# Output projection of a fused cross-attention and FFN kernel by seven block products per head pair, with its sums placed among the softmax steps

## What is computed

```python
x = x + xattn(layernorm(x), ctx, Wq, Wk, Wv, Wo)      # Wo: (16*128, 512)
#   scores = q k^T / sqrt(128); attn = softmax(scores); out = (attn v) @ Wo
x = x + ffn(layernorm(x), w_gate, w_up, w_down)       # silu(gate) * up, then down
```

## Time and profile before

| | us |
|---|---|
| median of 3 runs (lowest to highest) | 2036.09 (2035.24 to 2036.58) |
| the profiled execution: time / span in the profile | 2035.61 / 2034.0 |
| PE busy | 2016.0 (99%) |
| DVE / ACT / POOL busy | 1528.0 (75%) / 1001.8 (49%) / 739.9 (36%) |
| DMA, mean | 95 GB/s |

### The profile page before, as it was taken

How to read it: one execution, slowest core, us unless ns; L and a number is a source line. 1 busy time by engine, 2 the same in 40 slices (tenths; PEclk the granted TensorE clock), 3 DMA queues, 4 the chain that set the end, 5 groups by cost and what they waited for, 6 DMA issues and landing times.

```text
span 2034.0 us, 44904 instructions
## 1 busy us (share of the span) xinstructions
PE 2016.0 (99%) x15422; PEld 1508.8 (74%) x15422; DVE 1528.0 (75%) x3341; ACT 1001.8 (49%) x2679; POOL 739.9 (36%) x877
## 2 busy tenths in 40 slices
PE   8999999999999999999999999999999999999999
PEld 6888878788888887878888888888888885444444
DVE  6767777777777777777777777776656557899886
ACT  8955554554555545545554555545555443333332
POOL 5413333332333233333333333322111104878776
PEclk9999999999999999999999999999999999999999
DMA  8834344444444444444444354534233354555555
GB/s 253 219 63 92 83 97 87 84 92 91 88 89 91 92 91 86 87 89 91 87 81 102 73 105 77 104 71 94 53 84 58 68 133 98 91 87 94 93 91 99
DMA packets 456111, 193.74 MB, mean 95 GB/s; under 512 B 419456, under 2 KB 432256, under 8 KB 455904
## 3 DMA queue, kind: packets, MB, share of 16 engines
q1 hardware_dynamic: 433984, 140.31, 36.3%
q0 software_dynamic: 15584, 44.45, 8.8%
q10 hardware_dynamic: 6336, 6.29, 1.0%
HBM read 61.21 MB, written 27.26 MB: 43 GB/s over the span
## 4 chain that ended last, share of the span: by engine, by line
PE 93%; DVE 2%; DMA 2%; ACT 1%; issue 1%; POOL 0%; DVEq 0%; ACTq 0%; SPq 0%; POOLq 0%
PE b_qk L1085 33%; PE b_v L1085 17%; PE b_c L1085 10%; PE b_s L1085 9%; PE b_o L1140 8%; PE b_w L1140 8%; PE b_o L1211 3%; PE b_w L1211 2%; PE b_pt L1085 2%; PE b_x L1085 2%; DMA probT<-psplit 1%; ACT psplit L663 0%; DVE nmax L917 0%; ACT prob L653 0%; DVE kvT L755 0%
## 5 line engine op out<-in xcount | busy, mean ns | idle before, releaser
L1085 PE MATMUL b_qk<-kvT,attn_weights 128*128 128x256 f16 x3072 | 377.2, 273 | 3.7 <-DVE qk L755 2.9
L1085 PE MATMUL b_v<-attn_weights,kvT 128*128 128x256 f16 x3072 | 377.2, 273 | 0.0
L1085 PE MATMUL b_qk<-xT,attn_weights 128*128 128x256 f16 x3072 | 377.2, 273 | 0.0
L653 ACT ACTIVATE prob<-b_s,nmax 128x256 f32<-128x256 f32 x514 | 239.3, 470 | 278.2 <-DVE nmax L917 276.3
L1085 PEld LDWEIGHTS b_qk<-kvT,attn_weights 128*128 128x128 f16 x3072 | 300.2, 98 | 92.9 <-issue 5.1
L944 DVE SCALAR_TENSOR_TENSOR psplit<-prob,rrec,psplit 128x256 f16<-128x256 f32 x514 | 306.0, 636 | 79.6 <-ACT psplit L663 79.6
L755 DVE SCALAR_TENSOR_TENSOR qk<-b_qk,qk 128x512 f16<-128x512 f32 x256 | 176.7, 690 | 246.0 <-ACT qk L609 236.0
L609 ACT ACTIVATE qk<-b_qk 128x512 f16<-128x512 f32 x256 | 152.6, 596 | 423.4 <-PE b_qk L1085 423.0
L1085 PEld LDWEIGHTS b_qk<-xT,attn_weights 128*128 128x128 f16 x3072 | 300.6, 98 | 34.8
L1085 PEld LDWEIGHTS b_v<-attn_weights,kvT 128*128 128x128 f16 x3072 | 300.6, 98 | 34.8
L663 ACT ACTIVATE psplit<-prob,rrec 128x256 f16<-128x256 f32 x514 | 233.3, 501 | 69.2 <-DVE rrec L937 69.2
(11 more groups left out here) (131 smaller groups left out, 2685.8 us busy)
## 6 DMA issues: line engine op xcount, KB each, us to landing
ffn_w<-wffn SPq DMA_DIRECT2D x48, 256.0 KB, 2.8
acc<-xtok POOLq DMA_DIRECT2D x16, 512.0 KB, 4.7
out<-acc POOLq DMA_DIRECT2D x16, 512.0 KB, 3.3
xrow<-xtok POOLq DMA_DIRECT2D x31, 256.0 KB, 3.1
kvrow<-kvt POOLq DMA_DIRECT2D x61, 128.0 KB, 2.4
out<-attn_weights POOLq DMA_DIRECT2D x28, 256.0 KB, 5.4
stage<-wattn SPq DMA_DIRECT2D x12, 512.0 KB, 4.4
ffn_scratch<-ffn_t SPq DMA_DIRECT2D x48, 128.0 KB, 2.4
```

Source lines behind the costliest of these rows:

```text
L653: last = eng.activation(half(prob, q, 256), half(bS, q, 256), ACT.Exp, bias=nmax[:, q:q + 1], scale=1.0, accum_out=rsum[:, q:q + 1])
L1085: last = eng.matmul(out, l, r, start=(a == 0), stop=(a == len(pairs) - 1))
```

## The change

Pairs u = 0 to 15 (batches 0 and 1) are projected as before. From u = 16 (`FAST = 2`) a pair's product, (256 tokens x 256) times (256 x 512), is taken as a 2x2 block product and made from seven block products, each 128x128 times 128x256, instead of eight, from sums and differences of blocks (`TERMS`, m1 to m7). The parts:

- **PE**: `project_fast`: m1, m3, m4, m2 in even steps (12 matmuls of 256 columns into `b_pt` and `b_x`), m5, m7, m6 in odd steps (9, into `b_o` and `b_w`). A pair is projected one step later than before. The first pair of a batch from batch 3 waits by product for the sums of the previous batch (`m_step`, `READ`).
- **Left operand**: ACT leaves the context in fp32 (`evict_rows`), POOL forms five sums of blocks per pair (`left_sums`), ACT their hi (`left_hi`, 896 columns), DVE their lo (`left_lo`, 896 columns). Context lo per head goes away.
- **Right operand**: once, in quads 4 to 7: each of eight weight blocks is loaded, summed (POOL), split (ACT, DVE: `out_lo`) and stored in DRAM as 128x3584 fp16. Two blocks stay in SBUF after that, six per batch are loaded again (`load_slot`, 128x2048 and 128x1536), behind softmax transposes on SP's queue.
- **Sums into the rows**: 12 additions of 256 columns per batch (`add_products`) in place of two of 512, in groups of four behind the row maximum of heads 1, 2 and 3 of q = 1. For the last batch one addition per v = 0..11 of the FFN stage.
- **Moved**: FFN weight rounding runs in quads 8 to 55 (was 4 to 51); in q = 1 `ffn_magic` stands in head 3 (was 2); `x1_stats` stands in q = 2, head 1 (was q = 1, heads 2 and 3); `tile_rstd`, `store_x1`, `x_rescale` later in POOL's order. In the FFN stage two bank pairs serve until u = 27 (was 3), three after; ten downs stand at the end (was eight). SP's loops are written out.

```diff
+THIRD = 28
-GU_BUF = [u % 2 if u < 4 else (u - 2) % 3 for u in range(2 * PAIRS)]
+GU_BUF = [u % 2 if u < THIRD else (u - THIRD + 2) % 3 for u in range(2 * PAIRS)]
-NO_DOWN = (0, 1, 2, 3, 36, 40, 44, 48)
+NO_DOWN = (0, 1, 2, 3, 44, 47, 50, 53, 56, 59)
+TERMS = (("m1", "a0+b1", 3), ("m3", "a0", 2), ("m4", "b1", 1), ("m2", "a1+b1", 0)), \
+    (("m5", "a0+b0", 4), ("m7", "b0-b1", 6), ("m6", "a0-a1", 5))
+READ = {"m1": 4, "m3": 4, "m4": 8, "m2": 8, "m5": 11, "m7": 11, "m6": 12}
...
@@ gpsimd
+            def left_sums(n, k):
+                wait_apart(eng, "c_hi", 4 * n + k + 1)
...
+                eng.tensor_tensor(blocks[:, 4:6, :], blocks[:, 1:9:7, :], blocks[:, 0:4:2, :], ALU.add)
+                eng.tensor_tensor(blocks[:, 6:8, :], blocks[:, 0:2, :], blocks[:, 2:9:6, :], ALU.subtract)
+                eng.tensor_tensor(blocks[:, 3, :], blocks[:, 1, :], blocks[:, 2, :], ALU.add)
...
@@ scalar
+            def left_hi(n, k):
+                u = 2 * n + k // 2 - 2 - FAST_PAIR
+                eng.wait_ge(sm["s_sum"], 3 * (u + 1))
...
+                eng.activation(left_part(k // 2, 0).rearrange("p (n f) -> p n f", f=P), blocks[:, 1:8, :], ACT.Copy,
+                               scale=1.0).then_inc(sm["s_hi"], 1)
@@ vector
+            def left_lo(n, k):
+                eng.wait_ge(sm["s_hi"], 2 * n + k // 2 - 1 - FAST_PAIR)
+                eng.tensor_tensor(left_part(k // 2, 1).rearrange("p (n f) -> p n f", f=P), blocks[:, 1:8, :],
+                                  left_part(k // 2, 0).rearrange("p (n f) -> p n f", f=P), ALU.subtract
+                                  ).then_inc(sm["s_lo"], 1)
...
+            def add_products(b, group):
...
+                if group == 1:
+                    add_product(b, "m4", 1, 0, 0, 1)
+                    add_product(b, "m4", 1, 1, 0, None)
+                    add_product(b, "m2", -1, 1, 1, 4)
+                    add_product(b, "m2", 1, 1, 0, 6)
...
             def quad(...):
...
-                    if front or k < 3:
+                    sums = q == 1 and (not isinstance(s, int) or s > FAST)
+                    if sums and k > 0:
+                        add_products(s - 1, k - 1)
+                    if q == 2 and k == 1 and (not isinstance(s, int) or s > 0):
+                        for j in range(2):
+                            x1_stats(s - 1, j)
+                        x1_aggr(s - 1)
+                    if (front or k < 3) and not fast(n, k, 3):
...
-                    if ffn and k == 2:
+                    if ffn and k == 2 + sums:
                         ffn_magic(w)
...
@@ tensor
+            def project_fast(u, part):
...
+                for name, rows, block_ in TERMS[part]:
+                    at = LEFT[rows] * P
+                    if first_ and batch > FAST:
+                        eng.wait_ge(sm["m_step"], 12 * (batch - 1 - FAST) + READ[name])
+                    for z, (a, b) in enumerate(PARTS):
+                        last = eng.matmul(product_at[name], left_part(u % 2, a)[:, at:at + P], slot_w(slot, block_, b), ...)
@@ sync
+                    if QPB <= n < 2 * QPB and k % 2:
+                        j = 2 * (n - QPB) + k // 2
+                        store_out(j)
+                        if j < 7:
+                            load_out(j + 1)
+                    fill(i)
```

More of the change, by code:

```diff
@@ L366, in load_x_tile @@
                                         ).then_inc(sm[f"xqT_loaded{at}"], 16)
-            for n in range(NQ - 4, NQ - 1):
-                ffn_quad(n, store=False, load=False)
-            for k in range(QUAD):
-                transpose_p(4 * (NQ - 1) + k, k % 2)
-                if k < 2:
-                    load_x_tile(k, k)
+            begin = {0: 2 * 1 + 6, 4: 2 * 3 + 6, 1: 2 * 5 + 6, 2: 2 * 6 + 6}
+            fills = {}
+            for p_, step in begin.items():
+                for part in range(2):
+                    fills.setdefault(FAST_HEAD - 16 + step + part, []).append((FAST_PAIR + p_, part, FAST_HEAD - 20 + step))
@@ new lines, in _, with fill @@
+            order = [u for u in range(FAST_PAIR, B * H // 2) if u % 8 in RING]
+            for at, u in enumerate(order[2:]):
+                for part in range(2):
+                    old = order[at]
+                    fills.setdefault(2 * old + 6 + part, []).append((u, part, 2 * old + 1 + part))
+            def fill(i):
+                for u, part, done in fills.get(i, ()):
+                    eng.wait_ge(sm["o_done"], done)
+                    load_slot(u, part)
+            for n in range(NQ):
+                for k in range(QUAD):
+                    i = 4 * n + k
+                    w = n - FFN_FROM
+                    transpose_p(i, k % 2)
+                    if n % 2 and k == 1 and n < NQ - 4:
+                        transpose_x(n // 2)
+                    if n < QPB:
+                        for g in (EARLY + PIECES * n + 2 * k, EARLY + PIECES * n + 2 * k + 1):
+                            if PIECES <= g < QPB * PIECES - SLOTS:
+                                reload(g)
+                    if i == 4 * QPB - 1:
+                        load_out(0)
+                    if QPB <= n < 2 * QPB and k % 2:
[4 more added lines that the diff above has]
+                    fill(i)
+                    if i == 4 * FFN_FROM - 1:
+                        load_ffn(0)
+                    if FFN_FROM <= n < FFN_TO - 1 and k == 1:
+                        eng.wait_ge(sm["ffn_y"], w + 1)
+                        load_ffn(w + 1)
+                    if FFN_FROM < n <= FFN_TO and k == 2:
+                        transpose_ffn(w - 1)
+                    if FFN_FROM < n <= FFN_TO and k == 3:
+                        store_ffn(w - 1)
+                    if n == NQ - 1 and k < 2:
+                        load_x_tile(k, k)
@@ L374, in _ @@
             transpose_p(4 * NQ, 0)
+            fill(4 * NQ)
+            fill(4 * NQ + 1)
             def transpose_inner(v):
@@ new lines, in out_lo @@
+            def out_lo(j):
+                eng.wait_ge(sm["wo_hi"], 2 * j + 2)
+                to, hi_part = wo_part(1), wo_part(0)
+                pairs = [(to[:, 0:5:4, :], wo_rows[:, 0:4:3, :], hi_part[:, 0:5:4, :])]
+                for a in range(2):
+                    at = slice(1 + 4 * a, 3 + 4 * a)
+                    pairs.append((to[:, at, :], wo_sums[:, 2 * a:2 * a + 2, :], hi_part[:, at, :]))
+                pairs.append((to[:, 3, :], wo_cross, hi_part[:, 3, :]))
+                for dst, rows, above in pairs:
+                    last = eng.scalar_tensor_tensor(out=dst, in0=rows, scalar=W_SCALE, in1=above,
+                                                    op0=ALU.mult, op1=ALU.subtract)
+                last.then_inc(sm["wo_lo"], 1)
```

379 lines of the change are left out of this document (253 added, 126 removed).

## The result

The changed kernel takes **2049.11 us** (median of four runs, 2049.05 to 2051.06), the kernel before, beside it, 2035.66 (2034.66 to 2036.58): the ratio is **1.0069, with a 95% interval of 1.0056 to 1.0081**. It is slower by 13.5 us, in the runs and in the span (2047.5 for 2034.0). The forecast was 2020.0 us, between 2006 and 2036; it missed.

What follows compares the result with a forecast made beforehand. The prediction took PE, busy 99% of the span, as the bound. Its terms, -33.3 + 13 - 1.5 + 2 + 4.8 - 0.6 = -15.6 us from 2035.6, gave 2020.0 us, forecast 2012 to 2027, with rivals 2006 to 2036.

Steps and rivals of the forecast that it cites:

- Fewer columns, -33.3: PE's projection: 21 matmuls of 256 columns replace 12 of 512, saving 0.297 us a pair over 112 pairs, 33.3 us.
- rival E: Weight loads do not hide in PE's 256-column product groups: 99 us on top, about 2119; chance 0.01.
- Waits for the sums, +13: First pair of batches 3 to 15: PE waits for the previous batch's additions, about 1.0 us a batch, +13 us.
- Rival A: PE finds its banks free, so waits for the additions do not occur: 13 us kept, 2007; chance 0.14.
- DVE, ACT and POOL in the loop, -1.5: Attention head steps: added work on these engines costs 1.5 us, while 3 us of probT waits go; net -1.5.
- the cover of some 2.4: Slack in a head step: qk lo is due some 2.4 us before PE begins the next q and k.
- Rival C: POOL becomes the head step's bound through late left_sums of head 0: 39 us over 56 quads, 2057; chance 0.09.
- Preparing Wo, +2: Quads 4 to 7: eight load-sum-split-store rounds of 13.3 to 13.6 us, against 13.08 available, cost +2 us.
- Rival B: Wo preparation or the end costs its upper bound: +10 with transfers at 7.5 us, transition 4 more, 2028 to 2034; chance 0.15.
- Attention to FFN, +4.8 and -0.6: From last scores into FFN: PE waits 5.8 us, +4.8 net (2 to 9); the last down's wait goes, -0.6.
- Transfers, 0: Twelve weight loads per batch on SP's queue, ahead of probability transposes, cost nothing; without the two-step cover, 0 to 5.
- Rival D: Loads delay probability transposes beyond 7 us, so PE waits 1 us in each of 13 batches: 2033; chance 0.05.

Runs made afterwards that it cites:

- Experiment 9: Changed kernel with product m6 multiplied and added twice in every head pair, eight products instead of seven: 2072.5 us (1.0188).
- experiment 13: Changed kernel with the moves of experiment 1, experiment 3 and experiment 12, additions spread six, four, two, and x1 steps moved later: 2012.83 us (0.9887).
- experiment 4: Changed kernel with the additions of products m4, m2 and m5 to m7 each queued a head earlier in q = 1: 2036.2 us (1.0006).
- experiment 3: Changed kernel with POOL's left sums of the second pair ahead of tile_rstd in q = 2, from batch 3 on: 2036.5 us (1.001).
- experiment 6: Changed kernel with POOL's FFN rounding in q = 2 cut to 16 of 512 columns, results partly wrong: 2035.0 us (1.0004).
- experiment 2: Changed kernel with the x1 maximum of tile 0 moved from the third to the fourth head of q = 2: 2042.6 us (1.0042).
- experiment 1: Changed kernel with tile_rstd ahead of the second Wo sums in POOL's order of q = 2 in batch 1: 2041.4 us (1.003).
- experiment 12: Changed kernel with moves like experiment 1 and experiment 3, additions spread six, four, two, plus batch 1's next Wo load ahead of the store: 2014.2 us (0.9895).
- experiment 11: Changed kernel with moves like experiment 1 and experiment 3, additions spread six, four, two, plus out_lo behind the next head's maximum: 2031.8 us (0.9981).

## Why the prediction was wrong

By stretches of the two traces: batch 1 cost 10.8 us (to the start of batch 2: 230.26 for 219.51), batches 2 to 14 gained 3.6 (1360.25 for 1363.82), the last batch and the FFN stage cost 6.3. The sum is 13.5.

- **Fewer columns, -33.3: right.** Experiment 9 gives the price of a column, and ten batches of experiment 13 take 102.24 or 102.23 us where the earlier trace rows have 104.56: 0.29 us a pair for the 0.297 forecast. Weight loads hide in 256-column products too, so rival E is out.
- **Waits for the sums, +13: right.** PE waited 4.5 us before m4 and 9.4 before m5 over 13 batches (3 to 15) by matmul starts, 13.9 in all; 12.9 of them lie in batches 2 to 14. Rival A falls, and experiment 4 shows the cause to be the place of the additions.
- **DVE, ACT and POOL in the loop, -1.5: this step failed.** Batches 2 to 14 held 31.1 us of waits (1360.25 less 13 x 102.24), against 4.5 before (1363.82 less 13 x 104.56). Less the 12.9 of product waits that is 18.2 us, of which 12.1 before `b_qk` and 3.4 before `b_c` are at the one head behind q = 2. The working followed POOL through q = 3 to q = 0 and passed over q = 2, where the change itself puts `tile_rstd` ahead of the second sums. It priced a step with `left_lo` by its own length and never added the x1 apply and maximum that stand in the same step. And it used the lock-out only for psplit (1.48) and not for the apply, a longer instruction of the same kind next to the same rounding, which took 1.15 us in the kernel before already. Together they are 1.1 us over the cover of some 2.4; with the late sums or the stretch away, 0.1 to 0.2 is left in most batches (experiments 3 and 6), with the maximum away 0.4 (experiment 2). Rival C named the mechanism (POOL late, ACT and DVE behind it), but in head 0 of all 56 quads; it is head 2 of one quad in four, in 11 batches. The sign it gave, PE idle before `b_qk` released by DVE qk, is what the profile shows.
- **Preparing Wo, +2: this step failed too.** It cost 11.0. The closed loop was counted at 13.3 to 13.6 us a round, and rounds were issued 13.5 to 14.5 us apart, with one of 20.5 around the long wait. The forecast's own sum was loose as well: 0.4 us seven times, less a cover of 2.4, is 0.4 and not 2. What was left out is what else waits on POOL behind a sum that waits for a load: the order moved `tile_rstd` there, and that made 6.06 us (experiment 1), 1.85 of it at the lower clock. The landing behind the store, 5.5 us, was within the 6.1 allowed; experiment 12 shows what it was worth, 4.2 us in batch 1. Rival B's price (10 us) and its sign (batch 1 over 108 us) came true, but not its cause, transfers of 7.5 us.
- **Attention to FFN, +4.8 and -0.6: mechanism right, size a little low.** The two waits before `b_qk` were 2.02 and 1.16 (forecast 2.15 and 1.15), the last pair's 1.17 (1.05); the last down waits no more. All waits from the last head step to u = 8 come to 6.4 us by matmul starts, for 5.8. The stretch from the start of batch 15 on grew by 6.3 us, where the forecast's terms give 2.8 (4.8, less 0.6, less 2.4 of columns, plus 1.0 of product waits). Besides those 0.6 it holds two waits for `probT` in batch 15, 1.5 us together, and from the end of the last down (by matmul starts) to the end of the span it takes 4.8 us for 3.5. Why those two grew no run shows.
- **Transfers, 0: right.** PE's waits for `probT` are 5.1 us in 6 places, where the earlier trace rows has 4.6 in 5, with a DMA share of 0.60 for 0.42. Rival D is out. But the 3 us of them taken as gone were only partly had: by matmul starts they fell from 4.5 to 2.1 us in batches 2 to 14, and 1.5 us came up in batch 15.

Of the 29 us between -15.6 and +13.5, the loop term has 15 (18.2 of new waits less 4.5 old ones, for -1.5), Wo 9 and the last stretch 3.5; columns and product waits together are within 2. Both large misses come from not walking through q = 2.

## What to carry to other kernels

When a step is moved to another place on an in-order engine, walk through that very place on every engine, with all that already stands there. A mean over steps, or the one chain that looks worst, hides a single head that is over by 1 us in every batch. An item that waits for a load must have nothing behind it that another engine needs; a few tiny instructions queued there cost PE 6.7 us in one wait. And where several late items stack up in one step, it can be enough to move one of them out (experiment 3), if the place it goes to has room (experiment 2's had little).

## What the runs showed of the hardware

After the idle time of 6.65 us PE came back at half speed. Two windows behind it, the q-k group's halves (granted clock in the seventh place after the busy times):

```profile
202.27:204.78 2.51, 2.51 (x13) 1.72 (x13) 1.90 (x6) 1.81 (x7) 0.00 (x0) 0.50 0.00 0
204.78:206.74 1.96, 1.96 (x13) 1.50 (x12) 1.07 (x3) 1.96 (x5) 0.00 (x0) 0.66 0.00 0
```

The first twelve matmuls took 2.51 us for 1.31, at 1.2 GHz, the next twelve 1.96, then the clock was 1.00 again: 1.85 us on top of the wait. In experiment 11 a wait of 2.93 us before a context did the same, and more dearly: the context, scores and v groups behind it, 5.08 us long, all ran at 0.50, and about 2.9 us were lost. The context:

```profile
224.14:225.38 1.24, 1.24 (x7) 0.85 (x8) 0.88 (x2) 1.24 (x4) 1.08 (x2) 0.50 0.00 0
```

The waits of up to 1.75 us in batch 1 of experiment 1 left the clock at 1.00, and so did the one of 2.01 in batch 1 of experiment 11.

In the lock-out POOL's side is longer too. Beside `left_lo` and the apply, POOL's subtraction took 2.00 us (L563 above), and so it did in ten batches; the earlier trace rows has 1.33 for it, and in the other 38 cases it took 1.27 to 1.34.

An 896 KB store ahead of a 512 KB load on one queue cost the load 1.2 us, and the load ahead of the store cost the store 1.7 (experiment 12).
